# Gelu computed once on ScalarE, with the high parts of all eight chunks copied by VectorE

## The chip, the cores and the metric

The kernel runs on one core of one Trainium2 chip. The metric is the device time of one execution in microseconds (us). The kernel before was timed three times; its median is 812.7 us (811.55 to 813.7).

## The reference, cut to what matters

For 32 sequences (256 tokens of width 256, with a context of 77 rows of width 256 each), one cross-attention block is computed in fp32:

```
xq, ctx = layer_norm(x), layer_norm(context)
q = xq @ q_w;  k, v = split(ctx @ kv_w)              # 16 heads of 16
attn = softmax(where(mask, -max, q k^T / 4))
x = x + (attn v) @ proj_w + proj_b
h = layer_norm(x)
h = gelu(h @ fc1_w + fc1_b) @ fc2_w + fc2_b          # hidden width 1024, exact gelu
out = x + h
```

## The kernel before

**Tiling.** The 32 sequences are worked off as 16 pairs (j = 0 to 15, `pairs_of`). A pair has 512 tokens, which are four token tiles t of 128. The hidden width 1024 is eight chunks k of 128 (`HC` = 8).

**High and low parts.** Each fp32 product is made of three matmuls in the rounded type fp32r: high x high, high x low, low x high (`product`, L866; for the second MLP product lines 990 to 992). So every operand is kept as a high part (the value rounded to fp32r) and a low part (the value less its high part). For the hidden activations these are `g_hi` and `g_lo`, 128 x 512 for each chunk.

**The eight chunks of the MLP.** For chunk k, TensorE computes `fc1(j, k)` into one of four PSUM banks. ScalarE's `gelu(j, k)` applies gelu with the bias and writes fp32 into `g_f[k % 2]` in SBUF (L540); for k = 0 to 5 it applies it a second time, from the same bank, and writes `g_hi` (L542). For k = 6 and 7, VectorE makes `g_hi` by a copy from `g_f` (`g_high`, L723). VectorE's `g_low` (L726; the instruction is recorded at the helper's line, L594) subtracts `g_hi` from `g_f` and writes `g_lo`. There are two buffers `g_f`, so `gelu(j, k)` waits until `g_low(j, k - 2)` is done; chunk 7's `g_low` is issued in the next pair's body, behind that pair's `cT_split` and two `xT_split`.

**Order of the engines.** Every engine has its own program, whose order is written out by hand; semaphores join them.

- TensorE, around the change: `fc1` of eight chunks of pair j; then, in the body of the next pair, the transposes `cT` and `xT`, `scores` 0 and 1, three chunks of `fc2(j - 1, 0, k)`, `scores` 2 and 3, `k_proj`, `scores` 4 and 5, `attend(j, 0)`, `q_proj(j + 1, 0)`, and so on. (All indices j here are those of the body that issues them.) `xT(j + 1, 0)` waits for the seventh gelu of the pair before, `scores` 2 and 3 for `exp` 0 and 1, `k_proj` for `cT_split`, `q_proj` for both `xT_split`.
- ScalarE: the eight `gelu`, between chunks 2 and 3 `shift_rows` (L502), then a small activation that brings the table of exp in (L588), then `exp` (L508).
- VectorE: the last `row_max` and `shifts`, `g_low` 0, `v_values` (writes `V`), `g_low` 1, `normalise_ctx` (`cn`), `g_low` 2, `normalise_x` (`xa`), `g_low` 3 to 5, `g_high` 6, `g_low` 6, `g_high` 7; then `cT_split` (its first instruction is the reduce at L629) and the two `xT_split`, which read PSUM.
- SyncE: behind `shift_rows` it stores the shifts to DRAM (`sd`) and waits for that store, loads two rows of `QM` from it (which `scores` 0 waits for), and then issues the load of the next `xin` (L282).
- GpSimd: when `xin` has landed, `add_proj_b` (L423, 128 x 1024 in SBUF) and right behind it `add_fc2_b` (L428, the same size).

In pairs 0 to 13 VectorE's list is complete; pair 14 has no `normalise_ctx` and `normalise_x`; pair 15 has neither these nor `v_values` and the row maxima, and its `fc1` alternate with `fc2`.

Of the kernel before, what the change touches and what calls it, by code (L numbers as in the profile page):

```python
# [9 lines left out]
def xattn_block(nc, x, ctx, maskT, qn_w, qn_b, cn_w, cn_b, n2_w, n2_b, q_w, kv_w, proj_w, proj_b,  # L10
# [4 lines left out]
    ACT = mybir.ActivationFunctionType  # L15
# [17 lines left out]
    HC = HID // P  # L33
# [16 lines left out]
    with es:  # L50
        def sb(name, shape, dt=F32):
            return es.enter_context(nc.sbuf_tensor(name, shape, dt))

        def sem(name):
            return es.enter_context(nc.semaphore(name))
# [7 lines left out]
        bias = sb("bias", [P, 2 * G + HC])  # L63
# [52 lines left out]
        g_hi, g_lo = sb("g_hi", [P, HC, TN], F32R), sb("g_lo", [P, HC, TN], F32R)  # L116
# [17 lines left out]
        FC1 = (F[0], F[1], A[3], A[0])  # L134
# [78 lines left out]
        gelu_done = sem("gelu_done")  # L213
        g_hi_done = sem("g_hi_done")
# [8 lines left out]
        def least(n):  # L223
            return max(n, 0) if isinstance(n, int) else n
# [237 lines left out]
        def _(act):  # L462
# [72 lines left out]
            def gelu(j, k):  # L535
                act.wait_ge(f1_mm, HC * j + k + 1)
                act.wait_ge(g_lo_done, least(HC * j + max(k - 1, 0)))
                act.wait_ge(o_lo_done, NB * (j + 1))
                b1 = bias[:, 2 * G + k:2 * G + k + 1]
                act.activation(g_f[k % 2][:], FC1[k % 4][:], ACT.Gelu, bias=b1).then_inc(gelu_done, 1)  # L540
                if k < HC - 2:
                    act.activation(g_hi[:, k], FC1[k % 4][:], ACT.Gelu, bias=b1).then_inc(g_hi_done, 1)  # L542

            act.activation(KM[:].rearrange("p h b m -> p (h b) m"), pat_m[0:SROWS].to_broadcast([SROWS, H * NB, MX]),
                           ACT.Copy).then_inc(pat_done, 1)
# [46 lines left out]
        def _(dve):  # L592
            def low(dst, src, hi):
                return dve.tensor_tensor(dst, src, hi.bitcast(F32), ALU.subtract)  # L594
# [18 lines left out]
            def normalise_ctx(j):  # L613
                dve.wait_ge(rstd_step, 2 * (j + 1))
                for b in range(NB):
                    dve.tensor_scalar(cn[:, b], cn[:, b], moms[0:M, TT + b, 0:1], rstd[0:M, TT + b:TT + b + 1],
                                      ALU.subtract, ALU.mult).then_inc(cn_done, 1)
# [7 lines left out]
            def cT_split(j):  # L625
                dve.wait_ge(cT_mm, j + 1)
                dve.wait_ge(shift_stored, 16 * j)
                per_batch = cT_cols.rearrange("p k (b m) -> p (k b) m", m=MX)
                dve.tensor_reduce(per_batch[:, :, M:MX], per_batch[:, :, 0:M], X, ALU.add).then_inc(c_sum_done, 1)  # L629
                dve.wait_ge(c_sum_done, j + 1)  # L630
                dve.tensor_copy(cT_hi[:], cT_cols).then_inc(cT_hi_done, 1)
                dve.wait_ge(cT_hi_done, j + 1)
                low(cT_lo[:], cT_cols, cT_hi[:]).then_inc(cT_lo_done, 1)

            def xT_split(j, k):
                n = KC * j + KC - k
                dve.wait_ge(xT_mm, n)
                dve.tensor_copy(xT_hi[:, k], XT[k][:]).then_inc(xT_hi_done, 1)
                dve.wait_ge(xT_hi_done, n)
                low(xT_lo[:, k], XT[k][:], xT_hi[:, k]).then_inc(xT_lo_done, 1)  # L640
# [8 lines left out]
            def q_low(j, g):  # L649
                dve.wait_ge(q_hi_done, G * j + g + 1)  # L650
                dve.scalar_tensor_tensor(out=q_lo[:, g], in0=Q[g][:], scalar=bias[:, g:g + 1],
                                         in1=q_hi[:, g].bitcast(F32), op0=ALU.add, op1=ALU.subtract).then_inc(q_lo_done, 1)

            def v_values(j):
                dve.wait_ge(v_mm, j + 1)
                dve.wait_ge(pv_mm, NB * QUADS * j)
                dve.tensor_tensor(V[:, :, :, 0:D], VP[0:MX].rearrange("p (b h d) -> p b h d", b=NB, d=D),
                                  bv[:].rearrange("p (h d) -> p h d", d=D).unsqueeze(1).to_broadcast([MX, NB, H, D]),
                                  ALU.add).then_inc(v_done, 1)
# [9 lines left out]
            def shifts(j):  # L669
                dve.wait_ge(max_done, RBANKS * (j + 1))  # L670
                dve.tensor_scalar(shift[:, H], shift[:, 0], GONE, None, ALU.is_gt).then_inc(shift_done, 1)
                dve.wait_ge(shift_done, 2 * j + 1)
                dve.tensor_scalar(shift[:, 0:H], shift[:, 0:H], FLOOR, -1.0, ALU.max, ALU.mult).then_inc(shift_done, 1)
# [47 lines left out]
            def g_high(j, k):  # L721
                dve.wait_ge(gelu_done, HC * j + k + 1)
                dve.tensor_copy(g_hi[:, k], g_f[k % 2][:]).then_inc(g_hi_done, 1)  # L723

            def g_low(j, k):
                dve.wait_ge(gelu_done, HC * j + k + 1)  # L726
                dve.wait_ge(g_hi_done, HC * j + k + 1)
                low(g_lo[:, k], g_f[k % 2][:], g_hi[:, k]).then_inc(g_lo_done, 1)
# [63 lines left out]
            def body(j, par, mlp, prep, ahead):  # L792
                if prep:
                    cT_split(j + 1)
                    xT_split(j + 1, 1)
                    xT_split(j + 1, 0)
                if mlp:
                    g_low(j - 1, HC - 1)
                if prep:
                    k_low(j + 1)  # L800
                    q_low(j + 1, 0)
                if prep:
                    q_low(j + 1, 1)
                o_tokens(j, 0)
                o_columns(j, 0)
                if ahead:
                    ln_stats(j + 2)
                    ln_moments(j + 2)
                o_tokens(j, 1)
                o_columns(j, 1)  # L810
                if mlp:
                    add_x1(j - 1, 1 - par, 0)
                add_x(j, par, 0)
                h_moments(j, par, 0)
                if prep:
                    row_max(j + 1, 0)
                    row_max(j + 1, 1)
                add_x(j, par, 1)
                h_moments(j, par, 1)
                if prep:  # L820
                    row_max(j + 1, 2)
                h_normalise(j, par, 0)
                if prep:
                    row_max(j + 1, 3)
                h_normalise(j, par, 1)
                if prep:
                    for r in range(4, 8):
                        row_max(j + 1, r)
                if mlp and prep:
                    add_x1(j - 1, 1 - par, 1)  # L830
                hT_low(j, 0)
                hT_low(j, 1)
                if not prep:
                    add_x1(j - 1, 1 - par, 1)
                if prep:
                    for r in range(8, RBANKS):
                        row_max(j + 1, r)
                    shifts(j + 1)
                g_low(j, 0)
                if prep:  # L840
                    v_values(j + 1)
                g_low(j, 1)
                if ahead:
                    normalise_ctx(j + 2)
                g_low(j, 2)
                if ahead:
                    normalise_x(j + 2)
                for k in range(3, HC - 2):
                    g_low(j, k)
                g_high(j, HC - 2)  # L850
                g_low(j, HC - 2)
                g_high(j, HC - 1)
            pairs_of(dve, body)
            g_low(PAIRS - 1, HC - 1)
# [6 lines left out]
        def _(pe):  # L861
# [101 lines left out]

            def fc1(j, k):
                if k >= 4:
                    pe.wait_ge(g_hi_done, HC * j + k - 3)
                cols = slice(k * P, (k + 1) * P)
                product(FC1[k % 4][:], [((w1_hi[:, c, cols], w1_lo[:, c, cols]), (hT_hi[:, c], hT_lo[:, c]))
                                      for c in range(KC)]).then_inc(f1_mm, 1)
# [12 lines left out]

            def fc2(j, t, k):
                if t == 0 and k == 0:
                    pe.wait_ge(g_hi_done, HC * j + 6)
                if t == 0:
                    pe.wait_ge(g_lo_done, HC * j + k + 1)
                tok = slice(t * P, (t + 1) * P)
                dst = F[t // 2][:, (t % 2) * C:(t % 2 + 1) * C]
                pe.matmul(dst, g_hi[:, k, tok], w2_hi[:, k], start=(k == 0), stop=False)  # L990
                pe.matmul(dst, g_hi[:, k, tok], w2_lo[:, k], start=False, stop=False)  # L991
                last = pe.matmul(dst, g_lo[:, k, tok], w2_hi[:, k], start=False, stop=(k == HC - 1))  # L992
                if t % 2 and k == HC - 1:
                    last.then_inc(f2_mm, 1)
# [54 lines left out]
            def body(j, par, mlp, prep, ahead):  # L1049
# [41 lines left out]
                if mlp and prep:  # L1091
                    fc2(j - 1, 0, 3)
# [108 lines left out]
```

## Time and profile before

| | |
|---|---|
| median of three runs | 812.7 us |
| the profiled execution: its time | 810.04 us |
| its span, first to last instruction | 808.2 us |
| TensorE busy | 772.6 us (96%) |
| VectorE busy | 616.3 us (76%) |
| ScalarE busy | 560.1 us (69%) |
| GpSimd busy | 180.1 us (22%) |
| mean granted TensorE clock | 0.975 |

All times of the argument are from the one profiled execution, counted from the start of its span. A busy share says how full an engine is over the whole run; what decides is which engine waits for which at the place of the change. A row of the timeline gives the start, the duration, the engine, the line, the operation, the tile written and the tile read; "idle before" stands in brackets. A duration contains some 0.1 us that overlap with the next instruction of the same engine, so steps are taken from start to start. The pair shown is pair 7.

### The profile page before, as it was taken

To read this page: it belongs to the slowest core of one execution; us is meant where nothing else is said; L and a number is where in the kernel's file an instruction comes from. 1 tells how busy PE (TensorE), PEld (TensorE's weight loads), DVE (VectorE), ACT (ScalarE), POOL (GpSimd) and SP (SyncE) were. 2 spreads that over 40 slices of the span, in tenths; PEclk is the share of its full clock that TensorE was granted. 3 is DMA by queue.
4 is the path that set the end of the run, shared out by engine and by line. 5 is a ranking of instruction groups with operands and counts; after the bars stand their busy time and mean duration, and the time that the engine had idled before them with its cause. 6 is when DMAs were issued, how large, how long until landed. Compare 5 with 4: busy or idle time off the path is not lost.

```text
span 808.2 us, 16998 instructions
## 1 busy us (share of the span) xinstructions
PE 772.6 (96%) x5615; PEld 632.7 (78%) x5615; DVE 616.3 (76%) x1379; ACT 560.1 (69%) x781; POOL 180.1 (22%) x185
## 2 busy tenths in 40 slices
PE   5748999999999999999999999999999999999998
PEld 5635769788787978878797978879797887869687
DVE  6736778698787879878787887878787887878453
ACT  4617776778777677777677777767767777776832
POOL 2311122222202222220222222021222212121230
PEclk8659999999999999999999999999999999999999
DMA  8877659394775939385684938567493956739100
GB/s 238 155 112 148 76 152 144 115 142 111 145 120 142 128 116 147 102 163 104 153 115 139 131 109 154 106 150 109 139 141 124 139 118 136 106 110 149 32 28 26
DMA packets 89478, 100.47 MB, mean 124 GB/s; under 512 B 9060, under 2 KB 63576, under 8 KB 89432
## 3 DMA queue, kind: packets, MB, share of 16 engines
q1 hardware_dynamic: 88694, 99.55, 64.5%
q10 hardware_dynamic: 754, 0.53, 0.3%
q8 instruction: 17, 0.28, 0.2%
q14 instruction: 13, 0.11, 0.1%
HBM read 69.22 MB, written 30.83 MB: 124 GB/s over the span
## 4 chain that ended last, share of the span: by engine, by line
PE 73%; issue 10%; DMA 6%; ACT 4%; DVE 3%; POOL 2%; ACTq 0%; SPq 0%; DVEq 0%; POOLq 0%
PE A L866 20%; PE F L866 12%; PE ST L936 8%; PE A L945 7%; PE F L990 7%; PE F L992 6%; PE F L991 6%; PE ST L918 3%; DMA QM<-sd 2%; PE A L961 2%; DMA xin<-in_x 2%; PE A L918 1%; DMA raw_q<-in_L_xattn_q_w 1%; ACT QM L528 1%; DMA sd<-cT_lo 1%
## 5 line engine op out<-in xcount | busy, mean ns | idle before, releaser
L508 ACT ACTIVATE probs<-ST 78x512 f32<-78x512 f32 x256 | 137.3, 588 | 50.2 <-PE ST L936 48.3
L990 PE MATMUL F<-w_hi,g_hi 128*128 128x256 f32 x480 | 141.8, 295 | 0.0
L992 PE MATMUL F<-w_hi,g_lo 128*128 128x256 f32 x480 | 133.9, 279 | 0.0
L991 PE MATMUL F<-w_lo,g_hi 128*128 128x256 f32 x480 | 133.9, 279 | 0.0
L594 DVE TENSOR_TENSOR g_lo<-g_f,g_hi 128x512 fp32r<-128x512 f32 x128 | 107.1, 837 | 32.9 <-ACT g_hi L542 30.2
L528 ACT ACTIVATE QM<-mask_u 77x2048 fp32r<-77x2048 uint8 x64 | 116.9, 1898 | 0.0
L423 POOL TENSOR_TENSOR xin<-xin,projb 128x1024 f32<-128x1024 f32 x16 | 38.2, 2388 | 314.7 <-DMA xin<-in_x 314.7
L990 PEld LDWEIGHTS F<-w_hi,g_hi 128*128 128x128 f32 x480 | 90.3, 188 | 18.6 <-issue 18.5
L936 PE MATMUL ST<-QM,KM 127*78 127x256 f32 x512 | 93.5, 294 | 3.0 <-ACT probs L508 0.7
L434 POOL TENSOR_TENSOR oT_lo<-g_f,oT_hi 128x512 fp32r<-128x512 f32 x32 | 41.2, 1287 | 234.8 <-ACT oT_hi L515 234.8
L936 PEld LDWEIGHTS ST<-QM,KM 127*78 127x78 f32 x512 | 59.8, 146 | 40.3 <-ACT probs L508 33.3
L991 PEld LDWEIGHTS F<-w_lo,g_hi 128*128 128x128 f32 x480 | 90.5, 189 | 0.0
L992 PEld LDWEIGHTS F<-w_hi,g_lo 128*128 128x128 f32 x480 | 90.1, 188 | 0.0
L945 PE MATMUL A<-probs,V 78*32 78x256 f32 x1024 | 81.5, 391 | 0.0
L666 DVE TENSOR_REDUCE shift<-ST 128x6 f32<-128x462 f32 (+1 forms) x128 | 67.5, 569 | 18.3 <-PE ST L918 17.2
L540 ACT ACTIVATE g_f<-F,bias 128x512 f32<-128x512 f32 x64 | 44.1, 689 | 34.3 <-issue 20.2
L540 ACT ACTIVATE g_f<-A,bias 128x512 f32<-128x512 f32 x64 | 44.2, 690 | 20.2 <-PE A L866 14.4
L533 ACT ACTIVATE xT_hi<-A 128x512 fp32r<-128x512 f32 x32 | 17.4, 596 | 51.4 <-PE A L961 51.4
L866 PE MATMUL F<-xT_hi,w_hi 128*128 128x512 f32 x128 | 52.6, 411 | 0.3 <-DVE xT_lo L594 0.3
L866 PE MATMUL A<-xT_hi,w_hi 128*128 128x512 f32 x128 | 51.9, 405 | 0.0
L594 DVE TENSOR_TENSOR xT_lo<-A,xT_hi 128x512 fp32r<-128x512 f32 x64 | 42.7, 688 | 11.6 <-ACT xT_hi L533 10.5
L866 PE MATMUL A<-xT_lo,w_hi 128*128 128x512 f32 x128 | 50.7, 396 | 0.0
(168 smaller groups left out, 1843.5 us busy)
## 6 DMA issues: line engine op xcount, KB each, us to landing
QM<-qd SPq DMA_DIRECT2D x48, 512.0 KB, 14.6
xa<-in_x SPq DMA_DIRECT2D x16, 512.0 KB, 4.0
qd<-q_hi SPq DMA_DIRECT2D x32, 256.0 KB, 2.2
qd<-q_lo SPq DMA_DIRECT2D x32, 256.0 KB, 2.3
xin<-in_x SPq DMA_DIRECT2D x16, 512.0 KB, 5.0
QR<-qd SPq DMA_DIRECT2D x16, 480.0 KB, 5.2
out<-xin SPq DMA_DIRECT2D x30, 256.0 KB, 6.8
KM<-kd SPq DMA_DIRECT2D x48, 156.0 KB, 7.0
```

The lines of the kernel that those rows point to most:

```text
L434: pool.tensor_tensor(oT_lo[b][:].rearrange("p g n -> p (g n)"), oT[:], oT_hi[b][:].bitcast(F32).rearrange("p g n -> p (g n)"), ALU.subtrac ...
L508: act.activation(probs[:, quad % NSLOT, 2 * (p % 2):2 * (p % 2) + 2], ST[p % 2][0:MX].rearrange("p (h n) -> p h n", n=N), ACT.Exp, scale=S ...
L528: act.activation(QM[0:M, heads], mask_u8[:].rearrange("p b n -> p (b n)").unsqueeze(1).to_broadcast([M, H // MASK_PARTS, TN]), ACT.Copy).t ...
L540: act.activation(g_f[k % 2][:], FC1[k % 4][:], ACT.Gelu, bias=b1).then_inc(gelu_done, 1)
L594: return dve.tensor_tensor(dst, src, hi.bitcast(F32), ALU.subtract)
L666: dve.tensor_reduce(shift[:, 6 * c:6 * c + n, t], max_bank(r)[:, 0:n * MX].rearrange("p (h m) -> p h m", m=MX)[:, :, 0:M], X, ALU.max).the ...
L866: last = pe.matmul(dst, a, b, start=(n == 0), stop=(n == 3 * len(terms) - 1))
L936: last = pe.matmul(ST[p % 2][0:MX, i * N:(i + 1) * N], KM[:, h, b], QM[:, h, b * N:(b + 1) * N], start=True, stop=True)
L945: last = pe.matmul(A[2 * b + qq][32 * i:32 * (i + 1), g * N:(g + 1) * N], V[:, b, 4 * q + i], probs[:, quad % NSLOT, i], start=True, stop= ...
L990: pe.matmul(dst, g_hi[:, k, tok], w2_hi[:, k], start=(k == 0), stop=False)
L991: pe.matmul(dst, g_hi[:, k, tok], w2_lo[:, k], start=False, stop=False)
L992: last = pe.matmul(dst, g_lo[:, k, tok], w2_hi[:, k], start=False, stop=(k == HC - 1))
```

## The change

ScalarE no longer applies the second gelu: `gelu(j, k)` issues one instruction for every chunk. VectorE makes `g_hi` by a copy for all eight chunks, each right ahead of the `g_low` of the same chunk (chunk 7 as before). TensorE's two waits on `g_hi_done` become waits on `gelu_done`, with the same counts.

```diff
@@ ScalarE, gelu(j, k)
                 act.activation(g_f[k % 2][:], FC1[k % 4][:], ACT.Gelu, bias=b1).then_inc(gelu_done, 1)
-                if k < HC - 2:
-                    act.activation(g_hi[:, k], FC1[k % 4][:], ACT.Gelu, bias=b1).then_inc(g_hi_done, 1)
@@ VectorE, body
+                g_high(j, 0)
                 g_low(j, 0)
                 if prep:
                     v_values(j + 1)
+                g_high(j, 1)
                 g_low(j, 1)
                 if ahead:
                     normalise_ctx(j + 2)
+                g_high(j, 2)
                 g_low(j, 2)
                 if ahead:
                     normalise_x(j + 2)
-                for k in range(3, HC - 2):
+                for k in range(3, HC - 1):
+                    g_high(j, k)
                     g_low(j, k)
-                g_high(j, HC - 2)
-                g_low(j, HC - 2)
                 g_high(j, HC - 1)
@@ TensorE, fc1(j, k)
                 if k >= 4:
-                    pe.wait_ge(g_hi_done, HC * j + k - 3)
+                    pe.wait_ge(gelu_done, HC * j + k - 3)
@@ TensorE, fc2(j, t, k)
                 if t == 0 and k == 0:
-                    pe.wait_ge(g_hi_done, HC * j + 6)
+                    pe.wait_ge(gelu_done, HC * j + 6)
```

## Rows read from the trace of the kernel before

**Rows 1.** The page's first line.

```profile
span 808.2 us, 16998 instructions
```

**Rows 2.** Busy time of each engine in pair 7; last, TensorE's clock, DMA share, GB/s.

```profile
418.69:465.32 46.63, 46.30 (x347) 38.06 (x346) 38.50 (x85) 34.40 (x48) 10.57 (x10) 1.00 0.67 124
```

**Rows 3.** VectorE's copies of g_hi: count, busy us, mean ns, idle before.

```profile
L723 DVE CAST g_hi<-g_f 128x512 fp32r<-128x512 f32 x32 | 13.7, 427 | 6.8 <-ACT g_f L540 5.8
```

**Rows 4.** Timeline of ScalarE, pair 7: first gelu to first exp.

```profile
418.69 0.69 ACT L540 ACTIVATE g_f<-F,bias 128x512 f32<-128x512 f32 x1 [1.26 <-issue]
...
422.40 0.68 ACT L542 ACTIVATE g_hi<-A,bias 128x512 fp32r<-128x512 f32 x1
422.97 0.26 ACT L502 ACTIVATE cT_lo<-A 68x128 fp32r<-68x128 f32 x1
...
428.94 0.69 ACT L540 ACTIVATE g_f<-A,bias 128x512 f32<-128x512 f32 x1 [0.71 <-PE A L866]
...
431.06 1.06 ACT L508 ACTIVATE probs<-ST 78x512 f32<-78x512 f32 x2
```

**Rows 5.** Timeline of VectorE, pair 7: chunk 0 to the last chunk.

```profile
420.22 0.69 DVE L594 TENSOR_TENSOR g_lo<-g_f,g_hi 128x512 fp32r<-128x512 f32 x1
...
422.39 0.73 DVE L616 TENSOR_SCALAR cn<-cn,moms,rstd 77x256 f32<-77x256 f32 x2
423.18 0.69 DVE L594 TENSOR_TENSOR g_lo<-g_f,g_hi 128x512 fp32r<-128x512 f32 x1
...
425.08 0.68 DVE L594 TENSOR_TENSOR g_lo<-g_f,g_hi 128x512 fp32r<-128x512 f32 x1
...
428.26 0.43 DVE L723 CAST g_hi<-g_f 128x512 fp32r<-128x512 f32 x1
428.80 0.69 DVE L594 TENSOR_TENSOR g_lo<-g_f,g_hi 128x512 fp32r<-128x512 f32 x1
429.67 0.43 DVE L723 CAST g_hi<-g_f 128x512 fp32r<-128x512 f32 x1 [0.18 <-ACT g_f L540]
430.25 0.48 DVE L629 TENSOR_REDUCE A<-A 128x4 f32<-128x308 f32 x1 [0.16 <-issue]
...
434.33 2.44 DVE L594 TENSOR_TENSOR g_lo<-g_f,g_hi 128x512 fp32r<-128x512 f32 x1
```

**Rows 6.** Timeline of TensorE, pair 7: scores 0 and 1, scores 2 and 3, q_proj.

```profile
430.36 0.70 PE L936 MATMUL ST<-QM,KM 127*78 127x256 f32 x4 [0.31 <-DMA QM<-sd]
...
431.95 0.68 PE L936 MATMUL ST<-QM,KM 127*78 127x256 f32 x4
...
434.91 0.50 PE L866 MATMUL A<-xT_hi,qw_hi 128*128 128x512 f32 x1
```

**Rows 7.** Timeline of SyncE's load of xin and of GpSimd, pair 7.

```profile
425.96 0.45 SPq L282 DMA_DIRECT2D xin<-in_x  x1
...
431.49 2.39 POOL L423 TENSOR_TENSOR xin<-xin,projb 128x1024 f32<-128x1024 f32 x1 [20.58 <-DMA xin<-in_x]
433.83 2.39 POOL L428 TENSOR_TENSOR xin<-xin,fc2b 128x1024 f32<-128x1024 f32 x1
```

**Rows 8.** The same instruction of GpSimd in pairs 5 (earliest) and 10 (latest).

```profile
336.85 2.39 POOL L423 TENSOR_TENSOR xin<-xin,projb 128x1024 f32<-128x1024 f32 x1 [19.23 <-DMA xin<-in_x]
...
571.63 2.40 POOL L423 TENSOR_TENSOR xin<-xin,projb 128x1024 f32<-128x1024 f32 x1 [20.84 <-DMA xin<-in_x]
```

**Rows 9.** Timeline of setup, where GpSimd and VectorE both make low weights.

```profile
31.95 1.28 POOL L440 TENSOR_TENSOR w_lo<-raw_w,w_hi 128x512 fp32r<-128x512 f32 x1
...
31.95 2.96 POOL L440 TENSOR_TENSOR w_lo<-raw_w,w_hi 128x512 fp32r<-128x512 f32 x2
...
32.03 1.75 DVE L738 SCALAR_TENSOR_TENSOR w_lo<-raw_w,vecs,w_hi 128x512 fp32r<-128x512 f32 x1
```

**Rows 10.** Busy time of each engine in two stretches of pair 0.

```profile
78.00:80.00 2.00, 0.05 (x1) 0.00 (x0) 1.92 (x7) 1.99 (x2) 1.28 (x2) 1.00 1.22 137
81.70:83.40 1.70, 1.70 (x8) 1.51 (x7) 1.50 (x5) 1.70 (x2) 0.70 (x2) 0.50 1.08 123
```

## The prediction

> **What bounds the kernel now.** I read the page first, then the busy times of one pair, then the timelines of the four engines at the end of a pair's MLP. The profiled execution took 810.04 us, of which the span is 808.2 [rows 1]; it lies 0.3% below the median of the runs, 812.7. I make the sum against 810.04 and carry the difference over to the median. In pair 7 TensorE is busy for 46.30 of 46.63 us, at the full clock [rows 2]; VectorE has 38.50 and ScalarE 34.40. So TensorE's order is the critical path. Nothing that is taken off ScalarE shortens it by itself, and every new stall of TensorE adds in full, since no slack in a pair could take it back. The change therefore asks one question: does the copying on VectorE come in time for TensorE? The place where this is decided is the end of the chunks, from 418.69 (the first gelu of pair 7) to 434.91 (`q_proj` of the next pair).
>
> There VectorE is the engine without room. Between `g_low` 0 at 420.22 and the reduce of `cT_split` at 430.25 it has only short waits for gelus [rows 5]. What TensorE takes up next hangs on what comes after: `scores` 2 and 3 at 431.95 need exp 0 and 1, which begin at 431.06 [rows 4], `q_proj` at 434.91 needs both `xT_split`, which end as `g_low` 7 starts at 434.33 [rows 5, 6].
>
> **What the change removes.** Six activations of 0.68 us on ScalarE, in each of 16 pairs. From one gelu's start to the next step's there it is less: 422.40 to 422.97, 0.57 us [rows 4]. What this brings forward: `shift_rows`, by 0.57 us to 422.40, and behind it on SyncE the store of the shifts, the loads of `QM` and the load of `xin`, issued at 425.96 [rows 7]. `QM` is waited for once per pair, for 0.31 us before `scores` 0 in pair 7 [rows 6]. That is the most that the change can win there, and it wins it only where nothing later is late. The waits of `fc1` for a free bank get earlier too, but `fc1` doesn't stall now. Worth: nothing, as shown next.
>
> **What the change adds.** On VectorE six copies a pair. A copy takes 427 ns [rows 3], and the subtraction behind it starts 0.54 us after it (428.26 to 428.80 [rows 5]). I lay out the list anew with these steps: copy to its subtraction 0.54; subtraction to the next instruction 0.61; `V` 0.61 (a guess by the subtraction, the nearest row); `cn` 0.79 (422.39 to 423.18); subtraction 2 and `xa` together 1.90 (423.18 to 425.08) [rows 5]. From 420.22: chunk 0's copy 420.22, subtraction 420.76, `V` 421.37, copy 1 421.98, subtraction 422.52, `cn` 423.13, copy 2 423.92, subtraction 424.46, `xa`, then copy 3 at 426.36, and from there 1.15 per chunk: copy 4 427.51, copy 5 428.66, subtraction 5 429.20 to 429.89, copy 6 429.81, subtraction 6 430.35 to 431.04, copy 7 430.96. The reduce stood 0.58 behind copy 7 (429.67 to 430.25), so it comes at 431.54: 1.29 us late. The six steps are 3.24 us; the waits for gelus that they fill are the other 1.95.
>
> The two buffers `g_f` carry this back to ScalarE. Gelu 7 waits for subtraction 5, so with 0.1 us of signalling it starts at 429.99 in place of 428.94; table load and exp 0 follow 2.12 us later, at 432.11, 1.05 late [rows 4]. Exp 0 and 1 take 1.07, and `scores` 3 can't start before 433.25; both `scores` ended at 432.47, now at 433.51. So **TensorE stalls 1.04 us a pair** even with everything else in its favour. The late reduce alone is covered by that: `xT_split` ends 1.29 late, at 435.70, where `q_proj` would come at 434.91 + 1.04 = 435.95 [rows 5, 6].
>
> This holds for pairs 0 to 13. Pair 14 lacks `cn` and `xa` (2.1 us), which is more than the delay, and pair 15 runs at TensorE's pace of two products a chunk; I take 0 for both. Stalls by this chain alone: 14 x 1.05 = 14.7 us.
>
> `add_proj_b`, counted from the first gelu of its pair (the pairs begin 46.63 us apart [rows 2]), started in pairs 0 to 13 at 12.60, 11.48, 12.48, 12.31, 12.49, 11.44, 11.92, 12.80, 11.72, 12.28, 13.05, 11.91, 12.42, 12.34: fourteen rows, of which the earliest and the latest are [rows 8]. Less 0.57 each they lie between 10.87 and 12.48. On the same scale the new list has copy 6 at 11.12, subtraction 6 from 11.66 to 12.35, copy 7 from 12.27 to 12.70. Whoever asks first goes first, and where both ask again they alternate: in setup VectorE's instruction of 32.03 ended at 33.78, that is 0.55 behind GpSimd's first of 31.95 to 33.23, and GpSimd's second then lasted from 33.20 to 34.91, 1.71 in place of 1.28 [rows 9]. `add_proj_b` and `add_fc2_b` stand back to back, so:
> - Start after 12.35 (1 pair): GpSimd waits for copy 7, VectorE loses nothing; TensorE loses 1.05.
> - Start within subtraction 6 (8 pairs): copy 7 is held until GpSimd's first is through, at about 12.3 + 2.36 = 14.65. The reduce comes at 14.9 in place of 11.56, both `xT_split` end 4.08 later (430.25 to 434.33 [rows 5]) at 19.0, and `q_proj`, at 16.22 before, starts at 19.1: 2.9 us lost.
> - Start before that (5 pairs): subtraction 6 and copy 7, or copy 6 and subtraction 6, are each held once. From GpSimd's start at about 11.3: 2.36, 0.3 of the held instruction, 2.36, 0.5: the reduce comes at 17.0 and `q_proj` at 21.2: 5.0 us lost.
>
> Sum: 1.05 + 8 x 2.9 + 5 x 5.0 = 49 us. No row shows a copy held by GpSimd, so I bound it: if the copy isn't held, only subtraction 6 can be, which costs 2.9 in the five early pairs and 1.05 in nine, 24 us. I take the copy as held, since the nearest row is the subtraction's, and since at 427 ns for the same 512 elements it reads faster than the subtraction's 690. The second bound: GpSimd's two go through without letting VectorE in; then 13 pairs lose 5.0, 66 us.
>
> The Trainium skill speaks to this in "SBUF — State Buffer", section "Who interferes with whom": a copy or cast from SBUF to SBUF can run in a mode that uses the port pair shared with GpSimd, and then the two exclude each other for a whole instruction. No row here shows a copy held. By that rule the sum stays at 49; without it, at 24.
>
> **The clock.** In pair 0 TensorE was nearly idle from 78 to 80, and at 81.7 it was granted half the clock (1.2 in place of 2.4 GHz) until 85.1 [rows 10]. A pair of the third kind leaves it idle for 3.8 us between `scores` 3 and `k_proj`, as long as that idleness. Half the clock for 3.4 us costs up to 1.7 us of its work; I take 1.5 in each of five pairs, 7.5 us; bounds 0 and 13 x 1.5 = 20.
>
> Sum of the forecast: 810.04 + 49.3 + 7.5 = 866.8, and with the difference to the median about 869.
>
> **The rivals.**
> - *VectorE's late list alone* (chance 0.17). `xin` lands later than I think or GpSimd finds no gap, so that no collision reaches the splits. For it: 0.2 us later would already free some pairs. Against it: the load is issued from the same chain that the change brings forward. 812.7 + 14.7 = 827.
> - *The copy isn't held* (0.15): 812.7 + 24, or 837, up to 845 with some lost clock.
> - *Faster* (0.03). If the copies' steps fit into VectorE's waits, gelu 7 isn't late and TensorE only gains the wait for `QM`, 0.3 us in 15 pairs: 808. That decides if six steps cost under 1.95 us together, so under 0.33 each in place of 0.54. The copies' rows exclude nearly all of it.
> - *No change* (0.03): ScalarE's gain and VectorE's loss both hidden, 812.7. It needs the same short steps.
> - *Everything held twice, and the clock* (0.10): 66 + 20, about 895.
>
> **How the numbers follow.** My forecast, collisions of both kinds, has 0.52: its own range is 848 to 885. The range for 8 in 10 reaches down to the first rival and leaves out the last and what is under 826: 826 to 886. A change under 0.3% can't be told from none. Faster by more 0.03, within 0.03, slower 0.94.
>
> **What would show it.** Right: ScalarE some 65 us less busy, VectorE's copies 128 at 427 ns where not held; gelu 7 about 11.3 behind the first gelu of its pair; rows of copy 7 or subtraction 6 of 2 to 3 us while GpSimd adds; the stall of TensorE before `k_proj` and `q_proj`; `scores` 0 no longer waiting for `QM`. Wrong: copies of 427 ns beside a running `add_proj_b`; GpSimd's adds longer than 2.4 us in place of VectorE's; periods of a pair all near 47.7 (the first rival) or under 46.6.

## The result, and the profile after

The changed kernel took 845.87 us (median of four runs, 835.16 to 850.24) against 812.12 us before (811.55 to 813.7). The ratio is 1.0328 with a 95% interval of 1.0293 to 1.0364. It is formed without the two slower runs of the changed kernel (848.90 and 850.24), which lie over 1.5% above its fastest; by the medians it is 1.042. That spread turned out to be a part of the result. In a later session six more runs of the same kernel gave a median of 868.51 us (860.54 to 875.44), while the kernel before stayed at 811.66. My forecast was 869, with 826 to 886 as range: the direction was right, and the size, 57 us, was too large for the 34 of the first measurement.

The profiled execution is the fastest of the first four; the other three left no trace, so how many pairs were held up in them isn't known. The page's head:

```profile
span 833.3 us, 16998 instructions
...
PE 783.0 (94%) x5615; PEld 639.2 (77%) x5615; DVE 645.5 (77%) x1475; ACT 505.0 (61%) x685; POOL 182.4 (22%) x185
```

The span grew by 25.1 us. ScalarE lost 96 instructions and 55 us of busy time, VectorE got 96 more. The groups by form of VectorE, ScalarE and GpSimd at the place of the change (count, busy us, mean ns, idle before):

```profile
L592 DVE TENSOR_TENSOR g_lo<-g_f,g_hi 128x512 fp32r<-128x512 f32 x128 | 95.2, 744 | 11.9
L721 DVE CAST g_hi<-g_f 128x512 fp32r<-128x512 f32 x128 | 62.6, 489 | 9.4 <-ACT g_f L540 9.3
...
L540 ACT ACTIVATE g_f<-F,bias 128x512 f32<-128x512 f32 x64 | 44.2, 690 | 79.8 <-DVE g_lo L592 37.8 <-PE F L866 21.7 <-issue 20.2
...
L423 POOL TENSOR_TENSOR xin<-xin,projb 128x1024 f32<-128x1024 f32 x16 | 39.6, 2476 | 310.4 <-DMA xin<-in_x 310.4
```

Three things are new. ScalarE's gelus now wait for VectorE's subtractions (37.8 us for the banks F alone; before, no gelu waited for them). The copies have a mean of 489 ns where 427 stood in [rows 3], although a free copy takes 420: some are held. And GpSimd's first add has a mean of 2476 ns where it was 2.39 us in [rows 7, 8]: some of its adds are held as well.

Where the time went is seen best pair by pair. The busy times of pairs 6, 7, 11 and 12 (second column the length; of the last three the first is TensorE's granted clock), to be read against [rows 2]:

```profile
377.04:424.42 47.38, 46.45 (x347) 38.06 (x346) 39.07 (x91) 30.93 (x43) 10.62 (x10) 1.00 0.68 127
424.42:474.92 50.50, 48.27 (x347) 39.00 (x346) 40.81 (x91) 30.95 (x43) 10.72 (x10) 0.97 0.64 120
621.50:670.61 49.11, 46.85 (x347) 38.15 (x346) 40.79 (x91) 30.96 (x42) 10.93 (x10) 1.00 0.65 122
670.61:722.60 51.99, 49.76 (x347) 40.10 (x346) 40.80 (x91) 30.92 (x42) 10.84 (x10) 0.93 0.62 119
```

A pair took 46.63 us before. Ten of the fourteen pairs that I had counted are like pair 6, at 47.24 to 47.44. Four (7, 10, 11, 12) are long: 50.50, 51.85, 49.11 and 51.99. Above 46.63 each, the ten add up to 7.2 us and the four to 16.9, together the growth of the span but for 1 us. Three of the four (7, 10, 12) also ran at a lower granted clock of TensorE for a part of the pair; pair 11 did not.

**An undisturbed pair.** Timeline of ScalarE in pair 6:

```profile
377.04 0.69 ACT L540 ACTIVATE g_f<-F,bias 128x512 f32<-128x512 f32 x1 [1.27 <-issue]
...
385.75 0.69 ACT L540 ACTIVATE g_f<-F,bias 128x512 f32<-128x512 f32 x1 [1.74 <-DVE g_lo L592]
...
388.02 0.69 ACT L540 ACTIVATE g_f<-A,bias 128x512 f32<-128x512 f32 x1 [0.44 <-DVE g_lo L592]
...
390.13 2.28 ACT L508 ACTIVATE probs<-ST 78x512 f32<-78x512 f32 x4
```

and of VectorE:

```profile
381.38 0.73 DVE L614 TENSOR_SCALAR cn<-cn,moms,rstd 77x256 f32<-77x256 f32 x2
382.02 0.42 DVE L721 CAST g_hi<-g_f 128x512 fp32r<-128x512 f32 x1
...
388.37 0.69 DVE L592 TENSOR_TENSOR g_lo<-g_f,g_hi 128x512 fp32r<-128x512 f32 x1
388.98 0.42 DVE L721 CAST g_hi<-g_f 128x512 fp32r<-128x512 f32 x1
389.32 0.48 DVE L627 TENSOR_REDUCE A<-A 128x4 f32<-128x308 f32 x1
```

Counted from the pair's first gelu, gelu 7 comes at 10.98 (before: 10.25 [rows 4]), exp 0 at 13.09 (before: 12.37), copy 7 at 11.94 and the reduce at 12.28 (before: 11.56 [rows 5]). TensorE's row shows who is waited for:

```profile
390.75 0.95 PE L936 MATMUL ST<-QM,KM 127*78 127x256 f32 x4 [0.81 <-ACT probs L508]
```

The wait for `QM` before `scores` 0 [rows 6] is gone, and a longer one for exp stands before `scores` 2.

**A held pair.** VectorE, GpSimd and TensorE in pair 7:

```profile
436.36 2.60 DVE L721 CAST g_hi<-g_f 128x512 fp32r<-128x512 f32 x1
438.88 0.47 DVE L627 TENSOR_REDUCE A<-A 128x4 f32<-128x308 f32 x1
```

```profile
436.28 2.39 POOL L423 TENSOR_TENSOR xin<-xin,projb 128x1024 f32<-128x1024 f32 x1 [19.66 <-DMA xin<-in_x]
438.63 2.53 POOL L428 TENSOR_TENSOR xin<-xin,fc2b 128x1024 f32<-128x1024 f32 x1
```

```profile
440.44 0.34 PE L866 MATMUL A<-cT_hi,kvw_hi 128*128 128x156 f32 x1 [1.37 <-DVE cT_lo L592]
```

GpSimd's add began 0.08 us ahead of copy 7, and the copy took 2.60 in place of 0.42. Everything behind it on VectorE is 2.18 later than in pair 6, and TensorE waits for 1.37 us before `k_proj`. GpSimd's second add was held in turn until the copy was through (2.53 in place of 2.39). The rule of the Trainium skill that I had cited ("SBUF — State Buffer", "Who interferes with whom") is borne out: a copy from SBUF to SBUF and an add of GpSimd exclude each other. In pair 6 it was the other way round: the add asked at 389.19, in the middle of copy 7, and the copy lost nothing (the add's row is 2.45).

### The profile page after: what moved, and what is told of

The parts are those of the page before. It is cut to its first block, busy times and chain, and to the rows that moved or that the text cites. A ratio compares the mean times of both kernels' runs of the same rounds, so it can differ in the third digit from the quotient of the medians.

```text
span 833.3 us, 16998 instructions
## 1 busy us (share of the span) xinstructions
PE 783.0 (94%) x5615; PEld 639.2 (77%) x5615; DVE 645.5 (77%) x1475; ACT 505.0 (61%) x685; POOL 182.4 (22%) x185
## 4 chain that ended last, share of the span: by engine, by line
PE 42%; issue 31%; DVE 15%; POOL 4%; ACT 4%; DMA 3%; ACTq 1%; DVEq 0%; POOLq 0%; SPq 0%
PE A L866 13%; PE F L866 7%; PE ST L936 4%; PE A L945 4%; PE F L990 3%; PE F L992 2%; PE F L991 2%; DVE g_hi L721 2%; DVE shift L664 2%; DVE g_lo L592 2%; PE A L961 1%; DMA xin<-in_x 1%; PE ST L918 1%; POOL xin L428 1%; POOL rstd L419 1%
## 5 line engine op out<-in xcount | busy, mean ns | idle before, releaser
L936 PE MATMUL ST<-QM,KM 127*78 127x256 f32 x512 | 96.1, 299 | 12.9 <-ACT probs L508 12.2
L423 POOL TENSOR_TENSOR xin<-xin,projb 128x1024 f32<-128x1024 f32 x16 | 39.6, 2476 | 310.4 <-DMA xin<-in_x 310.4
L592 DVE TENSOR_TENSOR g_lo<-g_f,g_hi 128x512 fp32r<-128x512 f32 x128 | 95.2, 744 | 11.9
L936 PEld LDWEIGHTS ST<-QM,KM 127*78 127x78 f32 x512 | 61.5, 150 | 50.4 <-ACT probs L508 46.1
L540 ACT ACTIVATE g_f<-F,bias 128x512 f32<-128x512 f32 x64 | 44.2, 690 | 79.8 <-DVE g_lo L592 37.8
L721 DVE CAST g_hi<-g_f 128x512 fp32r<-128x512 f32 x128 | 62.6, 489 | 9.4 <-ACT g_f L540 9.3
L592 DVE TENSOR_TENSOR xT_lo<-A,xT_hi 128x512 fp32r<-128x512 f32 x64 | 42.8, 689 | 12.1 <-ACT xT_hi L533 10.9
```

Of the source, the lines that this page charges most:

```text
L936: last = pe.matmul(ST[p % 2][0:MX, i * N:(i + 1) * N], KM[:, h, b], QM[:, h, b * N:(b + 1) * N], start=True, stop=True)
```

## The experiments

"Held" means: an instruction whose row is 2.5 us or more in place of 0.42 (copy) or 0.69 (subtraction). Times "behind the first gelu" are counted in each pair. The kernel before, run beside them, had 812.71, 811.36 and 811.66 in the three sessions, each on another chip (experiments 1, 3 and 4; 2, 8 and the first of 6; 5, 7 and the second of 6).

**1. No add beside the copies (a_guard) and its control (b_guard).** In both, GpSimd's first add also waits for the last subtraction of the pair before.

```diff
             def body(j, par, mlp, prep, ahead):
+                if mlp:
+                    pool.wait_ge(g_lo_done, HC * j)
                 add_proj_b(j, par)
```

> The changed kernel, in which GpSimd's add_proj_b waits in addition until the eighth g_low of the pair before is done, so that no add can lie beside the last copies. Theory (late list plus random holds by GpSimd): copy 7 is 427 ns in all pairs, every pair of 0 to 13 takes 47.37 us as the undisturbed ones of the changed kernel did, so 14 x 0.74 = 10.4 us above the kernel before, 822 to 824, and little scatter between runs. Rival (the adds have no part in it, the loss is the late list and the loads): 835 to 850 with scatter as in the changed kernel.

> The kernel before with the same extra wait of add_proj_b. Both theories: g_low 7 is no longer held (0.69 in place of 1 to 2.9 us), TensorE's order doesn't notice, 811 to 813. It is the control for the wait itself: if it costs, a_guard has to be read against this run.

Measured: a_guard 821.72 (820.35 to 821.85), ratio 1.0101 (1.0079 to 1.0124). b_guard 811.47, ratio 0.9985 (0.9971 to 0.9999). The wait itself costs nothing. The instructions of VectorE on `g_hi` in a_guard (min/median/max ns):

```profile
L723 DVE CAST g_hi<-g_f x128: 412/420/430, 95.5 to 811.9; 128x512 fp32r<-128x512 f32 x128
L594 DVE TENSOR_TENSOR g_lo<-g_f,g_hi x128: 679/693/695, 96.0 to 812.4; 128x512 fp32r<-128x512 f32 x128
```

No instruction is held; the pairs 0 to 13 take 47.25 to 47.43 us and the runs lie within 0.2%. So the late list alone costs 9 us by the medians and 10 by the pairs (14 x 0.73), and what the changed kernel takes above 822, and its scatter, comes from GpSimd's adds, with what the clock takes behind them (5).

**2. What the 0.72 us of an undisturbed pair are (a_guard_buf3).** a_guard with a third buffer `g_f`.

```diff
+        g_f.append(hn[:, 0:2].rearrange("p t c -> p (t c)"))
...
-                act.wait_ge(g_lo_done, least(HC * j + max(k - 1, 0)))
+                act.wait_ge(g_lo_done, least(HC * j + max(k - 2, 0)))
...
-                act.activation(g_f[k % 2][:], FC1[k % 4][:], ACT.Gelu, bias=b1).then_inc(gelu_done, 1)
+                act.activation(g_f[k % 3][:], FC1[k % 4][:], ACT.Gelu, bias=b1).then_inc(gelu_done, 1)
```

> The changed kernel with the extra wait of add_proj_b (as in a_guard) and a third buffer g_f (it lies in the tile of the normalised h, which is dead by then), so that gelu k waits for subtraction k - 3 only. Theory (the 0.72 us that a_guard loses per pair is the late exp, held up through the two buffers): gelu 7 and exp 0 come on time (10.3 and 12.4 behind the first gelu); the list still ends 0.7 late, which leaves q_proj 0.2 late: 14 x 0.2, 814 to 816. Rival (the late reduce and splits alone cost the 0.72): 821 to 823 as a_guard.

Measured: 815.14 (814.16 to 817.64), ratio 1.0058 (1.0036 to 1.0079). Gelu 7 and exp 0 on ScalarE, and `q_proj` on TensorE, in the pair that began at 467.69:

```profile
477.95 0.69 ACT L543 ACTIVATE g_f<-A,bias 128x512 f32<-128x512 f32 x1 [0.72 <-PE A L869]
...
480.06 2.28 ACT L511 ACTIVATE probs<-ST 78x512 f32<-78x512 f32 x4
```

```profile
484.19 0.50 PE L869 MATMUL A<-xT_hi,qw_hi 128*128 128x512 f32 x1
```

Gelu 7 is back at 10.26 and exp at 12.37; `q_proj` comes at 16.50, where it stood at 16.22 before, since the list on VectorE is as late as it was. The pair takes 46.92 (the next one's first gelu is at 514.61). So of the 0.72 us some 0.43 were the exp held up through the two buffers, and the rest the late splits, hidden behind it.

**3. The list one instruction shorter (a_no_normx).** `normalise_x` of the pairs from 2 on works on two columns of 256; the other 254 are left out.

```diff
-                    normalise_x(j + 2)
+                    skip_normalise_x(j + 2)      # xa[:, t, 0:2] in place of xa[:, t]
```

> The changed kernel, in which normalise_x of the pairs from 2 on works on two columns of each tile only: it leaves out the normalisation of the other 254. This takes 1 us out of VectorE's list behind chunk 2. Theory: gelu 7 and copy 7 come on TensorE's time again (copy 7 at 11.0 behind the first gelu), ahead of every add, which start at 11.6 or later: no stall of 0.74, no hold, 809 to 813. Rival (copies cost in another way, such as ScalarE's waits for buffers at chunk 2 and 3): still 820 or more.

Measured: 815.18 (812.4 to 818.71), ratio 1.0026 (1.0005 to 1.0047). I had expected 809 to 813. The list got only 0.5 us shorter, not 1, since the small instructions cost too; copy 7 stood at 11.41. Undisturbed pairs took 46.82, a stall of 0.19 in place of 0.74, and in the profiled run, the slowest of the ten, only pair 2 was held (51.49; its add asked at 11.34). Half a microsecond on VectorE's list thus takes away three quarters of the stall and, in this profile, all holds but one. The mechanism stands; the stall didn't go to zero, because my number for the saving was too high.

**4. xin early, both adds in the midst of the list (a_early_xin).**

```diff
                 if prep:
+                    load_xin(j + 1, 1 - par)
                     spread_shift(sp, j + 1)
-                    load_xin(j + 1, 1 - par)
```

> The changed kernel, in which SyncE issues the load of the next xin ahead of the store and loads of the shifts. xin then lands 3 to 4 us earlier, at 8 to 9 us behind the first gelu of the pair, and both adds fall among copies and subtractions 4 to 7. Theory: each of the two adds holds one of VectorE's instructions for some 2.2 us, alternating, in every pair; the reduce comes at about 17 us behind the first gelu, a pair takes 5 us more than before, and 1.4 us more where the clock is halved: 880 to 905 us. Rival (an add only holds the copy, not the subtraction, or the holds overlap with waits): one hold a pair, 845 to 865.

Measured: 895.45 (892.28 to 896.64), ratio 1.1001 (1.0971 to 1.1031). VectorE and GpSimd in pair 5:

```profile
358.45 0.73 DVE L614 TENSOR_SCALAR cn<-cn,moms,rstd 77x256 f32<-77x256 f32 x2
359.10 0.41 DVE L721 CAST g_hi<-g_f 128x512 fp32r<-128x512 f32 x1
359.62 2.70 DVE L592 TENSOR_TENSOR g_lo<-g_f,g_hi 128x512 fp32r<-128x512 f32 x1
362.24 3.45 DVE L620 TENSOR_SCALAR xa<-xa,moms,rstd 128x256 f32<-128x256 f32 x4
```

```profile
358.88 2.90 POOL L423 TENSOR_TENSOR xin<-xin,projb 128x1024 f32<-128x1024 f32 x1 [12.55 <-DMA xin<-in_x]
361.73 2.85 POOL L428 TENSOR_TENSOR xin<-xin,fc2b 128x1024 f32<-128x1024 f32 x1
```

Each add holds one instruction, and VectorE gets one in between: subtraction 2 behind the first, one of the four of `normalise_x` (3.45 us in place of 1.38) behind the second. One thing doesn't fit strict turns: the first add's row begins at 358.88, while the second `cn` runs, and yet copy 2 (359.10) goes first and is not held; the add's 2.90 is 0.51 more than a free 2.39, so it started when the copy was nearly through. Pairs 7, 9 and 11 of this run show the same behind `cn`. In all copies 7 held, by contrast, the instruction in front was a subtraction. The adds came earlier than I had written (5 us, not 8 to 9), but two holds a pair put the reduce at 16.4 in most pairs, and the pairs at 51.4 to 52.9. Pair 14, which loses nothing elsewhere (39.16), took 50.63 here, with TensorE's mean clock at 0.80.

**5. One hold in every pair (a_early_wait).** As 4, with GpSimd's first add waiting for the eighth gelu, so that it asks at 11.8 behind the first gelu.

```diff
+                if mlp:
+                    pool.wait_ge(gelu_done, HC * j)
                 add_proj_b(j, par)
```

> The changed kernel with xin loaded ahead of the shifts (as in a_early_xin), and add_proj_b waiting until the eighth gelu of the pair before is done, at 11.7 behind the first gelu. GpSimd then asks while subtraction 6 runs (11.33 to 12.01), in every pair. Theory: copy 7 is held once in each of 14 pairs, its row is 2.4 to 2.6 us, the reduce comes at 14.4, and a pair takes 49.1 us at the full clock and up to 52.0 with the clock halved in part: 812 + 14 x (2.5 to 5.3), 847 to 886. Rival (the four long pairs of the changed kernel had another cause than the held copy): most pairs at 47.4, 822 to 835.

Measured: 875.23 (871.98 to 876.67), ratio 1.0771 (1.0746 to 1.0796). Copy 7 takes 2.60 us in each of the fourteen pairs, the reduce stands at 14.45 to 14.53. Three of these pairs:

```profile
349.78:398.90 49.12, 46.86 (x347) 38.17 (x346) 40.78 (x91) 30.95 (x43) 10.77 (x10) 1.00 0.65 124
398.90:450.87 51.97, 49.75 (x347) 40.08 (x346) 40.78 (x91) 30.91 (x43) 10.77 (x10) 0.93 0.61 117
554.70:605.26 50.56, 48.34 (x347) 39.00 (x346) 40.79 (x91) 30.96 (x43) 10.76 (x10) 0.97 0.63 119
```

The same hold costs 1.75 us above an undisturbed pair at the full clock (three pairs of the fourteen), and 3.2 (one pair) or 4.4 to 4.7 (ten) where TensorE's clock was at its lower level for a part of the pair (mean 0.97 and 0.93). The clock's part, up to 3.0 us, is larger than that of the hold. All fourteen pairs have the same idle time of TensorE; why three of them kept the full clock no run shows.

**6. Another form for copy 7 (a_slow_copy7, a_reduce_copy7).** First the addition of a zero from a column:

```diff
+                if k == HC - 1:
+                    dve.tensor_scalar(g_hi[:, k], g_f[k % 2][:], zero[:, 0:1], None, ALU.add).then_inc(g_hi_done, 1)
...
```

> The changed kernel, in which the copy of chunk 7 alone is made by another form of instruction: the addition of a zero that is read from an SBUF column (normalise_x's form, which takes 404 ns for 256 elements, so some 0.69 us for 512, against 0.42 of the copy). Theory (the copy is held because it runs at its fast rate, like an instruction with two operands in SBUF): this one is not held; it takes 0.69 us in every pair whatever GpSimd does, and each pair takes 47.4 to 47.6 us: 821 to 826, no scatter. Rival (GpSimd's add holds any instruction of VectorE between SBUF and SBUF): rows of 2.5 us and more in some pairs, 835 to 855 as the changed kernel.

Measured: 859.00 (858.47 to 875.51), ratio 1.0588 (1.0565 to 1.061), above both ranges. The premise failed: the form takes 0.48 us for 512 elements, so it runs nearly as fast as the copy, and it is held like it.

```profile
L724 DVE TENSOR_SCALAR g_hi<-g_f,zero x16: 478/1529/2600, 104.8 to 848.7; 128x512 fp32r<-128x512 f32 x16
```

This run says nothing on the question; it shows 8 held pairs of 14, two of them held twice. So then a reduce over an axis of length 1:

```diff
+                if k == HC - 1:
+                    dve.tensor_reduce(g_hi[:, k], g_f[k % 2][:].rearrange("p (n o) -> p n o", o=1), X, ALU.max).then_inc(g_hi_done, 1)
...
```

> The changed kernel, in which the copy of chunk 7 alone is made by a reduce with max over an axis of length 1, from SBUF to SBUF. The form with a zero from a column took 0.48 us for 512 elements, so it ran fast too and was held; a reduce of 462 elements takes 0.63 here, so I expect 0.65 to 0.70 for 512. Theory (only an instruction that runs fast or has two operands in SBUF is held): it is not held in any pair; the reduce of cT_split starts at 12.5 to 12.6 behind the first gelu in nearly every pair, a pair takes 47.4 to 47.7 us, 821 to 827. A subtraction 6 can still be held where GpSimd comes before 11.33. Rival (everything from SBUF to SBUF is held by an add): rows of 2.5 us, 835 to 860.

Measured: 834.33 (832.39 to 834.53), ratio 1.0268 (1.0249 to 1.0287). The instructions on `g_hi`:

```profile
L592 DVE TENSOR_TENSOR g_lo<-g_f,g_hi x128: 681/693/2694, 94.6 to 825.4; 128x512 fp32r<-128x512 f32 x128
L724 DVE CAST g_hi<-g_f x112: 410/420/430, 94.1 to 821.8; 128x512 fp32r<-128x512 f32 x112
L722 DVE TENSOR_REDUCE g_hi<-g_f x16: 672/679/687, 104.5 to 824.6; 128x512 fp32r<-128x512 f32 x16
```

All sixteen reduces take 0.67 to 0.69 us, though an add runs beside fourteen of them, as in pair 4 (VectorE, then GpSimd):

```profile
298.67 0.68 DVE L722 TENSOR_REDUCE g_hi<-g_f 128x512 fp32r<-128x512 f32 x1
```

```profile
298.44 2.54 POOL L423 TENSOR_TENSOR xin<-xin,projb 128x1024 f32<-128x1024 f32 x1 [19.51 <-DMA xin<-in_x]
300.94 2.38 POOL L428 TENSOR_TENSOR xin<-xin,fc2b 128x1024 f32<-128x1024 f32 x1
```

So an instruction from SBUF to SBUF with one operand isn't held as such: this reduce, which takes 0.68 us for the 512 elements, is not, and the two forms that take 0.42 and 0.48 are. The Trainium skill says the same of reduces in "SBUF — State Buffer", "Who interferes with whom". That it is the copy's fast form that makes it collide is the reading that fits; a slow copy of the same kind was not run. The time is above my 821 to 827 because in three pairs the add asked at 10.9, ahead of subtraction 6, which was held (2.68): these pairs took 52.17, 52.02 and 51.84, the other eleven 47.24 to 47.43.

**7. The changed kernel once more (a_again).** No edit.

> The changed kernel itself, for the scatter. Theory: the undisturbed pairs take 47.37 us and the time is 822 plus what the pairs with a held copy cost (1.7 us each, up to 4.6 with half the clock, more where two are held); the number of them goes by when xin lands and differs from run to run: 828 to 860, with a spread of over 1% where a_guard had 0.2%. Rival (a fixed loss): a spread of 0.3% about 846.

Measured: 868.51 (860.54 to 875.44), ratio 1.0667 (1.063 to 1.0705); above my 828 to 860, with a spread of 1.7%. In its profiled run four pairs are undisturbed, seven held once and three held twice. A pair of the last kind (length 55.13), VectorE and GpSimd:

```profile
297.03 2.87 DVE L592 TENSOR_TENSOR g_lo<-g_f,g_hi 128x512 fp32r<-128x512 f32 x1
299.83 2.58 DVE L721 CAST g_hi<-g_f 128x512 fp32r<-128x512 f32 x1
302.33 0.47 DVE L627 TENSOR_REDUCE A<-A 128x4 f32<-128x308 f32 x1
```

```profile
296.97 2.39 POOL L423 TENSOR_TENSOR xin<-xin,projb 128x1024 f32<-128x1024 f32 x1 [19.06 <-DMA xin<-in_x]
299.30 2.81 POOL L428 TENSOR_TENSOR xin<-xin,fc2b 128x1024 f32<-128x1024 f32 x1
```

The load of `xin` took 5.3 us from issue to landing (median) in the first profile and 5.0 here. 0.3 us, and six more pairs are held: in the first profile thirteen of the fourteen adds asked within 0.3 us of copy 7's start. Whether a chip has its own landing times isn't known: the changed kernel itself was timed in two sessions only.

**8. Fewer copies (b_guard_c2, b_guard_c012).** The kernel before with the extra wait of 1, and chunk 2 alone, or chunks 0 to 2, copied in addition to 6 and 7.

```diff
+        COPIED, TWICE = (2, 6, 7), (0, 1, 3, 4, 5)        # or (0, 1, 2, 6, 7), (3, 4, 5)
...
-                if k < HC - 2:
+                if k in TWICE:
                     act.activation(g_hi[:, k], FC1[k % 4][:], ACT.Gelu, bias=b1).then_inc(g_hi_done, 1)
...
+                g_high(j, 2)
                 g_low(j, 2)
```

> The kernel before with the extra wait of add_proj_b, and with chunk 2 alone copied by VectorE in addition to 6 and 7 (one second gelu fewer on ScalarE, the one that shift_rows waited behind). Theory: shift_rows comes 0.57 earlier, one copy of 0.54 fits into the waits of VectorE's list (1.95 us a pair), exp and splits stay on time, and the wait for QM before scores 0 is gone: 0.05 to 0.3 us a pair, 808 to 811. Rival (nothing to win there, or the copy is late): 811.5 as b_guard, or more.

> The same with chunks 0, 1 and 2 copied by VectorE, so three copies more than before and three fewer than changed. Theory: 1.6 us of copies against 1.95 us of waits: subtraction 3 is late, which reaches gelu 7 with 0.15 us at most; 810 to 813. Rival (each copy costs its share of the 9 us that six cost): 815 to 817.

Measured: 810.56 (ratio 0.9993, 0.9983 to 1.0003) and 810.85 (0.9993, 0.9981 to 1.0005). Neither can be told from the kernel before. One to three copies fit into VectorE's waits as reckoned, with exp 0 at 12.37 in both. But a pair still takes 46.65 us, although the wait for `QM` has gone from the list of waits. The 0.31 us were not to be won. In the kernel before, `scores` stood waiting for `QM` in two pairs only, 7 and 10 (0.6 us in all), and these two are as long as the others. As I read it (no run takes it apart), `scores` 3 waits for exp 1 in any case, and exp 1 hangs on gelu 7 and the table load, not on `QM`. None of the kernels tried beats the one before by more than b_guard's 0.15%.

## Why the prediction was right or wrong

**The wrong step: the count of collisions.** "They meet" was right; "1, 8 and 5 pairs" (none, one or two holds) was not. The first profile has 10, 4 and 0, the second 4, 7 and 3. That the count decides is shown by forcing it: 14, 0 and 0 gave 822 (a_guard), 0, 14 and 0 gave 875 (a_early_wait). Two errors of a few tenths lie behind it.
- Copy 7 was put at 12.27 and stands at 11.94. The step of `cn` was taken as 0.79 from 422.39 to 423.18 [rows 5], in which the subtraction's wait for ScalarE's second gelu (422.40 to 423.08 [rows 4]) was hidden; it is 0.64 (381.38 to 382.02). The step from a copy to its subtraction is 0.52, not 0.54, seven times ahead of copy 7, and the first copy starts 0.06 earlier. The order of an add and copy 7 thus flips in every pair whose add asks between 11.94 and 12.27: nine of the fourteen in the first profile.
- The adds asked at 12.1 in the median, 0.25 earlier than before, where I had moved them by the whole 0.57. The load was issued 0.57 earlier, as predicted (6.70 in place of 7.27, medians), but it took 0.3 longer in this run. What makes a load of 512 KB take 4.2 us in one pair and 5.7 in another of the same run (from the issue to the add's start, kernel before) isn't known, and I treated fourteen landing times of one run as if they were fixed.

With copy 7 put right and my adds left as they were, the count would have been 3 (after 11.94), 8 (from 11.33 on) and 3 (before), close to the second profile (there the adds asked at 11.8 in the median, 0.5 earlier than before). The first profile differs from that by its landings.

That the second session's 868.5 lies at my 869 is luck in part: at my own prices its 4, 7 and 3 pairs give 44 us, or 857, and the rest is clock that I hadn't counted (below). So is the agreement of the other sum: 10, 4 and 0 pairs at my prices give 22 us, or 835, which that execution took, but with a list and holds some 5 us too dear and a clock term of nothing in place of 7. The fair forecast would have been a wide one, with the sentence that 0.3 us of a transfer decide over 20 us.

**Terms of the sum.**
- The late list: 1.05 us a pair predicted, 0.74 measured, shown by a_guard (47.36 against 46.63). The chain was as described, by way of the two buffers and the exp (a_guard_buf3); the size is off by the same 0.3 of the list.
- One hold: 2.9 predicted, 2.48 measured (49.11 less 46.63).
- Two holds: the reduce at 17.0 predicted, 16.4 to 16.65 measured. The cost, 5.0 predicted at the full clock, can't be compared: the three such pairs (54.42 to 55.13) all ran in part at the lower clock and cost 7.8 to 8.5 with it. The order, GpSimd and VectorE in turns, read from the setup [rows 9], was right in these pairs; behind `cn` in a_early_xin it wasn't (4).
- Is the copy held: yes, and not for being SBUF to SBUF, since the reduce isn't (a_reduce_copy7). The step was a choice between 49 and 24 us, and it was taken rightly.
- The clock: 1.5 us in the pairs held twice, none in the others. Measured: also in pairs held once, above pair 11's 49.11, 1.4 in pair 7, 2.7 in pair 10 and 2.9 in pair 12. Before it TensorE was idle only for 0.8 us before `scores` 2 and 1.4 before `k_proj`; pair 11 had the same idle time and lost nothing. In the first profile this term is 7.0 of 25 us, near the 7.5 predicted, but from other pairs: that is luck. In the second it is 12.5 us in the pairs held once alone, and the pairs held twice, idle for 3.5 us before `k_proj` (3.8 predicted), have a mean clock of 0.91. Taking the term only for pairs held twice was the second wrong step.
- ScalarE's relief: 65 us of busy time predicted, 55 measured, since a second gelu overlapped the first by 0.1; it bought nothing, as said. The rival "faster" valued the wait for `QM` at 0.3 us in 15 pairs; it stands in two, and its worth is zero (b_guard_c2).
- Pairs 14 and 15: no loss, as predicted (39.16 and the same end).

**The rivals.** "The late list alone" would have been 827; with GpSimd kept away it is 822. The lower bound of the range held that case, and the first measurement lies between it and the forecast.

## What to carry to other kernels

Before work is moved to VectorE, look at what GpSimd does in the same microseconds, not at the busy shares: a copy from SBUF to SBUF and a subtraction of two SBUF operands each lost over 2 us here to one add of 128 x 1024. Where GpSimd's start hangs on a transfer, tie it to a point of VectorE's list by a semaphore, as a_guard does (b_guard shows that the wait costs nothing), or the kernel's time becomes a matter of landing times. And take steps for a new list only from rows that waited for nothing.

## What the runs showed of the hardware

- Where both engines had instructions waiting at the end of the chunks, they took turns, one each: in the pair held twice the first add ends at 299.36, the subtraction at 299.90, the second add at 302.11, the copy at 302.41. It is not a rule without exception: in a_early_xin a copy behind `cn` went ahead of an add whose row had begun 0.22 us before it. The held engine's row begins before the hold, so its duration (2.60, 2.87) is the sign to look for.
- An addition of a scalar from an SBUF column took 0.48 us for 512 fp32 elements and was held like a copy (0.42); a reduce over an axis of length 1 took 0.68 and never was.
- The lower clock of TensorE cost more than the hold ahead of it: one and the same hold made a pair 1.75 us longer at the full clock and 4.6 with a part of it at the lower one (a_early_wait). The same idle time came without a fall of the clock in three pairs of fourteen.
